# Pre-LN attention block with an fp8 linear layer: first batch's stacks by half heads, the second batch's projections inside the first batch's scores, one load behind the maxima's rows, and one sum of the tail moved from GpSimd to VectorE

## The chip, the cores and the metric

The kernel runs on one core of a Trainium2 chip. The metric is the device time of one execution in microseconds (us), the median of three runs. Engines are named as in the profile: PE is TensorE, PEld its weight loads, DVE is VectorE, ACT is ScalarE, POOL is GpSimd, SP is SyncE, which only issues DMAs here; SPq and ACTq are the issuing queues of SP and ACT.

## The reference

16 sequences of 512 tokens and 256 channels, 16 heads of 16 channels, all float32:

```
x = x + attention(layernorm(x))          # qkv projection, softmax(q k / 4) v, output projection
x = x + linear(fp8(layernorm(x)))        # input clipped to +-448 and rounded to fp8 e4m3, 256 x 256 weight, bias
```

## The kernel before, in words

**Slots and steps.** The work is a pipeline of batches: slot `u` prepares batch `u` (and x of batch `u+1`), runs the scores of batch `u-1`, finishes the exponentials and values of batch `u-2` and the linear layer of batch `u-3`. A slot has 32 steps `s`, written out by hand in each engine's program (PE L671, ACT L893, DVE L1122); tuples at the top of the file say at which step each side job stands (`PROJECT_QK_1`, `VALUES_AND_X`, `LN1_SUM`, `TRANSPOSE_MAX` and so on). Each engine runs its list in order, so a wait holds all that stands behind it.

**One step.** PE makes two score matmuls with queries on the partitions (`scores`, L628, into `ps_s[s % 2]`). DVE takes their maximum along the keys (`maxima`, L1013). After every 8 steps PE transposes these maxima (`transpose_max`, L534), DVE splits them into two rows (L1060, L1062), and SP copies them as two further contraction rows into the q stack (`rows`, L343: four DMAs of 4 KB). Half a slot later PE computes the same scores with keys on the partitions and the maximum already subtracted (`scores_t`, L609, into the two banks of `ps_t`), ACT takes their exponential into `pt` (L797), and PE multiplies with the values (`values`, L649) in every odd step. The scores of step `s` may start once the maxima of step `s-2` are done; `scores_t` of a bank may start once the exponential of the step before has read it.

**Precision by parts.** Projections are three products of high and low parts (6 matmuls for 128 columns). Q and K of a batch lie in `parts[:, n]`, n = 0 to 3: q and k of heads 0 to 7 (n = 0, 1) and of heads 8 to 15 (n = 2, 3). ACT takes n from its bank (L851), POOL splits it into high and low parts (L1330, L1332), and SP copies it into the `qs`/`ks` stacks by six DMAs of 128 KB (`stack`, L334). In the first batch, ACT (L848) and DVE (L1000) split, and n = 0 and 1 are copied by half heads with `copy_first` (L249, 64 KB each): the first four scores pairs need the semaphore `first_stack[0]`, 12 such DMAs. SP issues all of Q's, both halves of it, and K's second half (its `first_slot`); ACT issues K's first half, six DMAs (`stack_k`, L863), ahead of its copies of n = 2 and 3.

**Slot 0 on PE** (L494): transposes of x(0), `project_first` for n = 0 to 3, values of batch 0 (L515), then a wait until DVE has the last low part and ACT the values (`low_ready` 4, `v_ready` 4), 5 unread matmuls that only keep the engine busy (L506), and the 8 transposes of x(1) into `ps_o` and `ps_t` (L450). Then slot 1 begins. In its steps 0 to 15 there are no `scores_t`, only the scores of batch 0; one to three unread matmuls (L709) and one projection matmul of batch 1 (L464, `PROJECT_QK_1`) stand in each. n = 2 and 3 of batch 1 follow in steps 16 to 19 with three matmuls a step, all into the one bank `ps_m`. The values of batch 1 and the transposes of x(2) (`values_and_x`, L515 and L527) stand in steps 20, 22, 24 and 26. `scores_t` of batch 0 starts at step 16 and needs the rows of steps 0 to 7 (`rows_in[0]`).

**Layernorm of x(2)**: DVE takes the sums (L1020) and moments (L1026 to L1030) in slot 0, before the first maxima; POOL takes the power and normalises x(2) (`layernorm_x`, L1287, L1298) early in slot 1, before its splits of batch 1. In all later slots the sums stand at steps 5, 7, 10, 12 and 13.

**SP in slot 1**: the load of x(3) (L314), rows 0, stack n = 0, stack n = 1, rows 1, stacks n = 2 and 3, rows 2. ACT issues the six K DMAs of heads 8 to 15 of batch 0 (L889) at the end of its slot 0.

**The tail** (`finish`): the last batch is rounded to fp8 on DVE in three pieces of 2, 1 and 1 token blocks (`LAST_PIECES`), five DVE operations a piece (L1250 to L1260); each piece is transposed by PE (L770), copied by ACT (L947), multiplied by PE (L780); then DVE scales and adds (L1266) and SP stores. POOL adds the second half of the batch before (L1465, two operands in SBUF, 128x512) once ACT has scaled it (L938).

Of the kernel before, what the change touches and what calls it, by code (L numbers as in the profile page):

```python
# [5 lines left out]
F32 = mybir.dt.float32  # L6
# [48 lines left out]
PROJECT_QK_1 = (range(4, 10), range(10, 16), (16, 17), (18, 19))  # L55
# [9 lines left out]
LN1_END = 13  # L65
LN2_SUM = (31, 31, 1, 2)
# [5 lines left out]
WARM_STEPS = (2, 2, 2, 2, 1, 1, 1, 1, 3, 1, 1, 1, 1, 1, 1, 1)  # L72


def block_kernel(nc, x, qkv_wT, qk_bT, v_bT, proj_wT, proj_b, lin_wT, lin_b, in_scale, w_scale, eye, out):
# [4 lines left out]
    with ExitStack() as ctx:  # L80
# [181 lines left out]

        def sum_bank(half):

            return (ps_o, ps_m)[half][:].rearrange("p (j d) -> p j d", j=2)
# [26 lines left out]
        def _(sp):  # L292
# [58 lines left out]
            def first_slot():  # L351

                load(2, 0)
                sp.wait_ge(ones, 1)
                for par in range(2):
                    for g in range(2):
                        rows = slice(HALF * g + KR, HALF * g + KM)
                        sp.dma_start(ks[par][rows, :, :].bitcast(F32),
                                     nmax[:].rearrange("p t i m -> p (t i m)")).then_inc(ks_ones, 16)
                for half in range(2):  # L360
                    sp.wait_ge(whole_ready, 1)
                    for r in (0, 1):
                        copy_first(sp, qs, 0, Q_PARTS, r, half)
                    sp.wait_ge(low_ready, 1)
                    copy_first(sp, qs, 0, Q_PARTS, 2, half)
                sp.wait_ge(low_ready, 2)
                for r in (0, 2, 1):
                    copy_first(sp, ks, 1, K_PARTS, r, 1)
                stack(0, 0, 2)

            def slot(u, par, present):
                if u == 0:
                    first_slot()
                    return
# [12 lines left out]
                if present(2, B - 1):  # L387
                    reload(u - 2, par)
                if present(3) and u < LAST_SLOT:
                    store(u - 3, 0)  # L390
                if present(1):
                    rows(u - 1, 1 - par, 1)
                if present(3) and u < LAST_SLOT:
                    store(u - 3, 1)
                if present(0):
                    stack(u, par, 2)
                    stack(u, par, 3)
                if present(1):
                    rows(u - 1, 1 - par, 2)
# [17 lines left out]
        def _(pe):  # L417
# [35 lines left out]
            def project_qk(u, n, part, parts):  # L453

                bank = ps_m[:]
                if part == 0:
                    take_bank("project_qk", n, u)
                    if n == 0:
                        pe.wait_ge(xnT_low, 2 * u + 2)
                first = (n % 2) * D + (n // 2) * P  # L460
                products = [(pw, px, c) for pw, px in PAIRS for c in range(NC)]
                for m in range(6 * part // parts, 6 * (part + 1) // parts):
# [27 lines left out]
            def first_slot():  # L490
# [142 lines left out]
            def values(b, par, n, a):  # L633

                t, odd, kp = n // 4, n // 2 % 2, n % 2
                if a == 0:
                    if n == 0:
                        pe.wait_ge(v_ready, NJ * b + NJ)

# [15 lines left out]
            def slot(u, par, present):  # L655
# [3 lines left out]
                for s in range(STEPS):  # L659
# [11 lines left out]
                    if s in TRANSPOSE_MAX[:3] and present(1):  # L671
                        transpose_max(u - 1, TRANSPOSE_MAX.index(s))
                    if u == 1 and s < len(WARM_STEPS):
                        unread(WARM_STEPS[s])
# [10 lines left out]
                    if s in VALUES_AND_X and present(0):  # L685
                        values_and_x(u, VALUES_AND_X.index(s))
# [19 lines left out]
            def unread(count):  # L706

                for i in range(count):
                    nc.tensor.matmul(ps_t[:, 1, :], wqkv_p[:, 0, 0, 0:P], wqkv_p[:, 0, 0, 0:S], start=True, stop=True)  # L709
# [78 lines left out]
        def _(act):  # L788
# [48 lines left out]
            def copy_qk(b, par, n):  # L837

                t, bias = n // 2, bias_column(b, n)
                bank = ps_s[:, n // 2, n % 2, :] if isinstance(b, int) and b == 0 else ps_m[:]  # L840
# [22 lines left out]
            def stack_k(half):  # L863

                act.wait_ge(whole_ready, 2)
                for r in (0, 2):
                    copy_first(act, ks, 1, K_PARTS, r, half)
                act.wait_ge(low_ready, 2)
                copy_first(act, ks, 1, K_PARTS, 1, half)

            def first_slot():
# [6 lines left out]
                stack_k(0)  # L878
# [4 lines left out]
                for c in range(NC):  # L883
                    copy_xnT(1, c)
                act.wait_ge(low_ready, 4)
                for r, part in enumerate(K_PARTS):
                    for g in range(2):
                        rows = slice(HALF * g + HD * r, HALF * g + HD * (r + 1))
                        act.dma_start(ks[0][rows, NS:2 * NS, :].bitcast(F32),  # L889
                                      parts[HALF * g:HALF * (g + 1), 3, part, :]).then_inc(stacked[1][0], 16)  # L890

            def slot(u, par, present):
# [3 lines left out]
                for s in range(STEPS):  # L896
# [14 lines left out]
                    if s in VALUES_AND_X and present(0):  # L911
                        copy_v(u, par, VALUES_AND_X.index(s))
                        if u < B - 1:
                            copy_x_half(u + 1, VALUES_AND_X.index(s))
# [49 lines left out]
        def _(dve):  # L964
# [5 lines left out]
            def prepare():  # L970
# [33 lines left out]
                for j in range(NJ):  # L1004
                    ln1_sum(2, 0, j)
                ln1_finish(2)
# [126 lines left out]
            def slot(u, par, present):  # L1133
                for s in range(STEPS):
# [54 lines left out]
            def finish(b):  # L1189
# [71 lines left out]
                for n, (low, high) in enumerate(LAST_PIECES):  # L1261
# [5 lines left out]
                                             in1=h[:, tok, :], op0=ALU.mult, op1=ALU.add).then_inc(y_ready, 1)  # L1267

# [11 lines left out]
        def _(pool):  # L1280
# [112 lines left out]
            def slot(u, par, present):  # L1393
# [3 lines left out]
                if u == 1:  # L1397
# [3 lines left out]
                    layernorm_x(2, 0)  # L1401
# [16 lines left out]
                if present(-1) and u != 1:  # L1418
# [37 lines left out]
            def finish(b):  # L1456
                for half in range(2):
# [47 lines left out]
```

## Time and profile before

| | |
|---|---|
| median of 3 runs | 931.93 us (931.64 to 932.08) |
| the profiled execution | 932.24 us |
| its span in the trace | 930.4 us |
| PE busy | 912.7 us, 98% of the span |
| DVE, ACT, POOL busy | 836.2, 667.5, 514.4 us (90, 72, 55%) |
| granted TensorE clock | 1.00 of full |
| DMA, mean over the span | 85 GB/s |

The profiled execution is 1.84 us longer than its span (launch and end around it) and 0.31 us above the median. Times in trace rows count from the span's start. "Idle before" names the time that the engine stood still before a row and what released it.

### The profile page before, as it was taken

To read this page: it belongs to the slowest core of one execution; us is meant where nothing else is said; L and a number is where in the kernel's file an instruction comes from. 1 tells how busy PE (TensorE), PEld (TensorE's weight loads), DVE (VectorE), ACT (ScalarE), POOL (GpSimd) and SP (SyncE) were. 2 spreads that over 40 slices of the span, in tenths; PEclk is the share of its full clock that TensorE was granted. 3 is DMA by queue.
4 is the path that set the end of the run, shared out by engine and by line. 5 is a ranking of instruction groups with operands and counts; after the bars stand their busy time and mean duration, and the time that the engine had idled before them with its cause. 6 is when DMAs were issued, how large, how long until landed. Compare 5 with 4: busy or idle time off the path is not lost.

```text
span 930.4 us, 17052 instructions
## 1 busy us (share of the span) xinstructions
PE 912.7 (98%) x5901; PEld 434.3 (47%) x5901; DVE 836.2 (90%) x1264; ACT 667.5 (72%) x1294; POOL 514.4 (55%) x528
## 2 busy tenths in 40 slices
PE   7999999999999999999999999999999999998997
PEld 5444444445444454544445444444544445443336
DVE  6978899898999989899998989999898998899986
ACT  3277767777776777777777777777777677776784
POOL 4533449285573937638294664829556492833433
PEclk9999999999999999999999999999999999999999
DMA  7864607556281644718355380745538064470101
GB/s 199 139 104 85 100 25 132 74 76 111 52 142 38 120 66 79 127 37 144 52 104 81 66 143 24 143 66 91 93 59 142 10 127 59 66 118 3 47 1 47
DMA packets 46206, 78.92 MB, mean 85 GB/s; under 512 B 10088, under 2 KB 13288, under 8 KB 46120
## 3 DMA queue, kind: packets, MB, share of 16 engines
q1 hardware_dynamic: 45352, 76.65, 46.7%
q10 hardware_dynamic: 768, 1.18, 0.8%
q8 instruction: 47, 0.77, 0.4%
q14 instruction: 39, 0.32, 0.1%
HBM read 17.90 MB, written 8.39 MB: 28 GB/s over the span
## 4 chain that ended last, share of the span: by engine, by line
PE 93%; DVE 3%; ACT 2%; DMA 1%; issue 1%; SPq 0%; POOL 0%; ACTq 0%; DVEq 0%; POOLq 0%
PE ps_t L609 28%; PE ps_o L649 27%; PE ps_m L464 10%; PE ps_s L628 8%; PE ps_m L515 6%; PE ps_m L550 5%; PE ps_m L584 3%; ACT pt L797 2%; PE ps_s L534 1%; PE ps_m L527 1%; DVE mx L1013 1%; PE ps_m L567 1%; PE ps_s L486 1%; DMA qs<-nmax 1%; DMA xin<-in_x 0%
## 5 line engine op out<-in xcount | busy, mean ns | idle before, releaser
L797 ACT ACTIVATE pt<-ps_t 128x512 f32<-128x512 f32 x1008 | 548.8, 599 | 187.5 <-PE ps_t L609 183.6
L1013 DVE TENSOR_REDUCE mx<-ps_s 128x2 f32<-128x1024 f32 x512 | 611.5, 1207 | 43.0 <-PE ps_s L628 40.9
L609 PE MATMUL ps_t<-qs,ks 50*128 50x512 f32 x1008 | 375.5, 449 | 7.0 <-ACT pt L797 6.8
L628 PE MATMUL ps_s<-ks,qs 48*128 48x512 f32 x1024 | 375.1, 450 | 0.0
L609 PEld LDWEIGHTS ps_t<-qs,ks 50*128 50x128 f32 x1008 | 159.8, 184 | 286.4 <-ACT pt L797 206.0
L649 PE MATMUL ps_o<-pt,vt 128*32 128x512 f32 x2048 | 272.4, 604 | 0.0
L1341 POOL TENSOR_TENSOR on<-ot,rden 128x256 f32<-128x256 f32 x63 | 39.1, 621 | 225.5 <-DVE rden L1074 225.5
L628 PEld LDWEIGHTS ps_s<-ks,qs 48*128 48x128 f32 x1024 | 158.4, 184 | 6.6 <-DVE mx L1013 4.0
L464 PE MATMUL ps_m<-xnT_p,wqkv_p 128*128 128x512 f32 x360 | 109.1, 420 | 0.1
L1332 POOL TENSOR_TENSOR parts<-parts 128x512 f32<-128x512 f32 x60 | 81.6, 1360 | 4.9
L649 PEld LDWEIGHTS ps_o<-pt,vt 128*32 128x32 f32 x2048 | 40.5, 108 | 88.2 <-issue 81.8
L464 PEld LDWEIGHTS ps_m<-xnT_p,wqkv_p 128*128 128x128 f32 x360 | 60.9, 188 | 33.7 <-issue 25.2
L1316 POOL TENSOR_TENSOR oT_p<-oT,oT_p 128x512 fp32r<-128x512 f32 x31 | 39.7, 1280 | 47.0 <-ACT oT_p L835 47.0
L851 ACT ACTIVATE parts<-ps_m,b_qk 128x512 f32<-128x512 f32 x60 | 41.3, 688 | 30.7 <-PE ps_m L464 30.6
L515 PE MATMUL ps_m<-wqkv_p,xnT_p 128*128 128x256 f32 x360 | 58.1, 296 | 0.1
L550 PE MATMUL ps_m<-wproj_p,oT_p 128*128 128x256 f32 x360 | 54.2, 293 | 0.0
L515 PEld LDWEIGHTS ps_m<-wqkv_p,xnT_p 128*128 128x128 f32 x360 | 46.2, 188 | 14.8 <-issue 14.3
L550 PEld LDWEIGHTS ps_m<-wproj_p,oT_p 128*128 128x128 f32 x360 | 45.5, 189 | 10.1 <-issue 10.1
L1308 POOL CAST xnT_p<-xn 128x512 fp32r<-128x512 f32 x30 | 18.4, 612 | 54.5 <-PE ps_m L515 52.0
L1070 DVE STREAM_TRANSPOSE ot<-ps_o 128x512 f32<-128x512 f32 x63 | 44.2, 702 | 1.4 <-PE ps_o L649 1.4
L1330 POOL CAST parts<-parts 128x512 fp32r<-128x512 f32 x60 | 36.6, 609 | 14.6 <-ACT parts L851 14.6
L1372 POOL TENSOR_TENSOR hn<-hn,xres 128x1024 f32<-128x1024 f32 x14 | 33.3, 2381 | 12.8 <-DVE xres L1102 12.8
(145 smaller groups left out, 836.3 us busy)
## 6 DMA issues: line engine op xcount, KB each, us to landing
qs<-parts SPq DMA_DIRECT2D x186, 128.0 KB, 4.4
ks<-parts SPq DMA_DIRECT2D x180, 128.0 KB, 5.2
xin<-in_x SPq DMA_DIRECT2D x16, 512.0 KB, 3.6
xres<-in_x SPq DMA_DIRECT2D x15, 512.0 KB, 5.7
out<-h SPq DMA_DIRECT2D x29, 256.0 KB, 2.6
qs<-nmax SPq DMA_DIRECT2D x256, 4.0 KB
pt<-in_qkv_wT SPq DMA_DIRECT2D x1, 768.0 KB, 5.2
qs<-parts SPq DMA_DIRECT2D x12, 64.0 KB, 3.4
```

The costliest lines, as they stand in the source:

```text
L464: last = nc.tensor.matmul(bank, wqkv_p[:, pw, c, first:first + P], xnT_p[:, px, c, :], start=m == 0, stop=m == 5)
L515: last = nc.tensor.matmul(bank, xnT_p[:, px, c, tok], wqkv_p[:, pw, c, 2 * D:3 * D], start=(m == 0 and c == 0), stop=(m == 2 and c == NC - 1))
L550: last = nc.tensor.matmul(bank[:, j * D:(j + 1) * D], oT_p[:, px, t, tok], wproj_p[:, pw, t, :], start=(m == 0 and t == 0), stop=(m == 2 a ...
L609: nc.tensor.matmul(t_bank(b, s, g), ks[par][rows, slot, keys], qs[par][rows, slot, :], start=True, stop=True).then_inc(st_done, 1)
L628: done = nc.tensor.matmul(ps_s[:, s % 2, g, :], qs[par][rows, slot, queries], ks[par][rows, slot, :], start=True, stop=True)
L649: last = nc.tensor.matmul(ps_o[32 * i:32 * i + VW, :], vt[par][:, 2 * kp + a, head, :], pt[n % 2][:, i, a, :], start=(kp == 0 and a == 0), ...
L797: nc.scalar.activation(pt[n % 2][:, w % 2 + 2 * a, w // 2, :], t_bank(b, s, a), ACT.Exp, scale=SCALE).then_inc(exp_done, 1)
L851: nc.scalar.activation(parts[:, n, 1, :], bank, ACT.Identity, bias=bias).then_inc(whole_ready, 1)
L1013: dve.tensor_reduce(mx[:, r, :, s % QUARTER], ps_s[:, s % 2, :, :], AX_X, ALU.max).then_inc(max_done, 1)
L1070: dve.transpose(ot[:].rearrange("p a c -> p (a c)"), ps_o[:]).then_inc(ot_ready, 1)
L1316: pool.tensor_tensor(oT_p[:, 1, t, :], oT[:], oT_p[:, 0, t, :].bitcast(F32), ALU.subtract).then_inc(oT_low, 1)
L1332: pool.tensor_tensor(parts[:, n, 1, :], parts[:, n, 1, :], parts[:, n, 0, :], ALU.subtract).then_inc(low_ready, 1)
```

## The change

Steps and banks of slot 1: batch 1's projections get three steps of two matmuls each in steps 5 to 16, by turns into `ps_m` and `ps_o`, with the products ordered by the half of x that they need; the transposes of x(1) move from the end of slot 0 into steps 1 and 2; `values_and_x` moves to 22, 24, 26, 28; unread matmuls in slot 1 fall from 22 to 11. The 5 unread matmuls of slot 0 write `ps_o` and no longer wait. ACT's first-half K copy shrinks from six DMAs to two, and SP issues the other four, after Q's first half and ahead of Q's second; ACT's K copies of the second heads follow its copy of the transposed x(1). The sums for x(2) move on DVE from slot 0 to steps 15 to 19 of slot 1, and POOL's normalising of it behind its four splits. SP takes rows 0 ahead of the load of x(3). In the tail DVE makes the sum of L1465 after its first piece. Only slots 0 and 1 and the tail are touched.

```diff
-PROJECT_QK_1 = (range(4, 10), range(10, 16), (16, 17), (18, 19))
+PROJECT_QK_1 = ((5, 6, 7), (8, 9, 10), (11, 12, 13), (14, 15, 16))
+TRANSPOSE_X_1 = (1, 2)
+VALUES_AND_X_1 = (22, 24, 26, 28)
+LN1_SUM_1 = (15, 16, 17, 18)
+LN1_END_1 = 19
-WARM_STEPS = (2, 2, 2, 2, 1, 1, 1, 1, 3, 1, 1, 1, 1, 1, 1, 1)
+WARM_STEPS = (2, 0, 0, 2, 2, 0, 0, 0, 1, 0, 0, 0, 0, 0, 0, 4)
...
+        def qk_bank(b, n):
+
+            if b == 0:
+                return ps_s[:, n // 2, n % 2, :]
+            return ps_o[:] if b == 1 and n % 2 else ps_m[:]
...
-                for half in range(2):
-                    sp.wait_ge(whole_ready, 1)
-                    for r in (0, 1):
-                        copy_first(sp, qs, 0, Q_PARTS, r, half)
-                    sp.wait_ge(low_ready, 1)
-                    copy_first(sp, qs, 0, Q_PARTS, 2, half)
+                sp.wait_ge(whole_ready, 1)
+                for r in (0, 1):
+                    copy_first(sp, qs, 0, Q_PARTS, r, 0)
+                sp.wait_ge(low_ready, 1)
+                copy_first(sp, qs, 0, Q_PARTS, 2, 0)
                 sp.wait_ge(low_ready, 2)
+                copy_first(sp, ks, 1, K_PARTS, 1, 0)
+                copy_first(sp, ks, 1, K_PARTS, 2, 0)
+                for r in (0, 1, 2):
+                    copy_first(sp, qs, 0, Q_PARTS, r, 1)
                 for r in (0, 2, 1):
                     copy_first(sp, ks, 1, K_PARTS, r, 1)
                 stack(0, 0, 2)
...
+                if u == 1:
+                    rows(0, 0, 0)
                 if present(-2):
                     load(u + 2, par)
-                if u == 1:
-                    rows(0, 0, 0)
...
-                bank = ps_m[:]
+                bank = qk_bank(u, n)
                 if part == 0:
-                    take_bank("project_qk", n, u)
-                    if n == 0:
+                    if u > 1 or n % 2 == 0:
+                        take_bank("project_qk", n, u)
+                    if u > 1 and n == 0:
                         pe.wait_ge(xnT_low, 2 * u + 2)
+                    if u == 1 and n == 1:
+                        pe.wait_ge(xnT_ready, 6)
+                    if u == 1 and n == 3:
+                        pe.wait_ge(whole_ready, 4 + 2)
...
+                    if u == 1 and n == 0 and m % 3 == 0:
+                        pe.wait_ge(xnT_low, 2 + c + 1)
...
-                pe.wait_ge(low_ready, 4)
-                pe.wait_ge(v_ready, 4)
                 for i in range(WARM_SCORES):
-                    nc.tensor.matmul(ps_s[:, 1, 1, :], wqkv_p[:, 0, 0, 0:P], wqkv_p[:, 0, 0, 0:S], start=True, stop=True)
-                for c in range(NC):
-                    transpose_x(1, c)
+                    nc.tensor.matmul(ps_o[:], wqkv_p[:, 0, 0, 0:P], wqkv_p[:, 0, 0, 0:S], start=True, stop=True)
...
+                    if u == 1 and s == TRANSPOSE_X_1[1]:
+                        pe.wait_ge(v_ready, 4)
+                    if u == 1 and s in TRANSPOSE_X_1:
+                        transpose_x(1, TRANSPOSE_X_1.index(s))
...
-            def stack_k(half):
+            def stack_k():
 
                 act.wait_ge(whole_ready, 2)
-                for r in (0, 2):
-                    copy_first(act, ks, 1, K_PARTS, r, half)
-                act.wait_ge(low_ready, 2)
-                copy_first(act, ks, 1, K_PARTS, 1, half)
+                copy_first(act, ks, 1, K_PARTS, 0, 0)
...
+                    if u == 1 and s in TRANSPOSE_X_1:
+                        copy_xnT(1, TRANSPOSE_X_1.index(s))
+                    if u == 1 and s == TRANSPOSE_X_1[1]:
+                        stack_second_k()
...
                 finish_bias()
-                for j in range(NJ):
-                    ln1_sum(2, 0, j)
-                ln1_finish(2)
...
-                    if present(-1) and u > 1:
-                        if s in LN1_SUM:
-                            ln1_sum(u + 1, 1 - par, LN1_SUM.index(s))
-                        if s == LN1_END:
+                    if present(-1) and u > 0:
+                        steps_sum, step_end = (LN1_SUM_1, LN1_END_1) if u == 1 else (LN1_SUM, LN1_END)
+                        if s in steps_sum:
+                            ln1_sum(u + 1, 1 - par, steps_sum.index(s))
+                        if s == step_end:
                             ln1_finish(u + 1)
...
+                    if n == 0:
+                        dve.wait_ge(lin_scaled, 1)
+                        dve.tensor_tensor(y_before[:, 2:4, :], y_before[:, 2:4, :], xin[0][:, 2:4, :],
+                                          ALU.add).then_inc(y_before_ready, 1)
...
                     split_lin()
-                    layernorm_x(2, 0)
...
-                if present(-1) and u != 1:
+                if present(-1):
                     layernorm_x(u + 1, 1 - par)
...
-                pool.wait_ge(lin_scaled, 1)
-                pool.tensor_tensor(y_before[:, 2:4, :], y_before[:, 2:4, :], xin[0][:, 2:4, :],
-                                   ALU.add).then_inc(y_before_ready, 1)
```

## Rows read from the trace of the kernel before

**Rows 1.** The page's chain that ended last, share by engine

```profile
PE 93%; DVE 3%; ACT 2%; DMA 1%; issue 1%; SPq 0%; POOL 0%; ACTq 0%; DVEq 0%; POOLq 0%
```

**Rows 2.** Timeline of PE, end of slot 0: start us, us, instruction, idle before

```profile
17.39 3.15 PE L515 MATMUL ps_t<-wqkv_p,xnT_p 128*128 128x256 f32 x24
21.36 1.39 PE L506 MATMUL ps_s<-wqkv_p 128*128 128x512 f32 x5 [0.81 <-ACT vt L811]
...
23.55 0.50 PE L628 MATMUL ps_s<-ks,qs 48*128 48x512 f32 x2
```

**Rows 3.** Timeline of SP: DMA issues in slots 0 and 1

```profile
13.50 7.60 SPq L249 DMA_DIRECT2D qs<-parts  x12
...
25.10 5.59 SPq L334 DMA_DIRECT2D qs<-parts  x6
```

**Rows 4.** Tile ks: ACT's last two issues of K's first half, at 17.6 and 18.3

```profile
DMA to landing us min/median/max: 4.2/4.7/5.2
```

**Rows 5.** Tile ks, 21.0 to 22.5 us: three issues of SP, ACT issuing none

```profile
DMA to landing us min/median/max: 2.7/2.8/3.0
```

**Rows 6.** Tile qs: SP's last issue of the second heads' Q, at 29.8

```profile
DMA to landing us min/median/max: 9.5/9.5/9.5
```

**Rows 7.** Chain in order of time: the wait for the rows of steps 0 to 7

```profile
36.47 6.04 DMA qs<-nmax
```

**Rows 8.** Timeline of DVE, slots 0 and 1

```profile
21.66 1.41 DVE L1020 BATCH_NORM_STATS2 st<-xin 128x6 f32<-128x256 f32 x4 [0.26 <-POOL xn L1298]
...
23.70 0.15 DVE L1030 TENSOR_REDUCE ve<-mv 128x4 f32<-128x8 f32 x1
24.10 9.14 DVE L1013 TENSOR_REDUCE mx<-ps_s 128x2 f32<-128x1024 f32 x8 [0.25 <-PE ps_s L628]
...
43.62 0.28 DVE L1060 TENSOR_SCALAR nmax<-ps_s 16x128 fp32r<-16x128 f32 x1 [0.37 <-PE ps_s L534]
...
44.15 2.33 DVE L1013 TENSOR_REDUCE mx<-ps_s 128x2 f32<-128x1024 f32 x2
```

**Rows 9.** Timeline of POOL, slot 1: normalising x(2)

```profile
30.80 1.02 POOL L1287 TENSOR_TENSOR rs<-ve,half_neg 128x4 f32<-128x4 f32 x1
32.15 2.16 POOL L1298 TENSOR_SCALAR xn<-xin,nm,rs 128x256 f32<-128x256 f32 x4 [0.33 <-POOL rs L1287]
```

**Rows 10.** Timeline of PE: first scores_t of steps 23, 26, 28 and 30 of slot 1

```profile
54.62 0.50 PE L609 MATMUL ps_t<-qs,ks 50*128 50x512 f32 x1
...
59.75 0.50 PE L609 MATMUL ps_t<-qs,ks 50*128 50x512 f32 x1
...
63.19 0.50 PE L609 MATMUL ps_t<-qs,ks 50*128 50x512 f32 x1
...
66.36 0.50 PE L609 MATMUL ps_t<-qs,ks 50*128 50x512 f32 x1
```

**Rows 11.** Timeline of the tail: DVE, POOL and PE around the second and third pieces

```profile
919.63 0.69 DVE L1258 TENSOR_TENSOR hn<-hn,parts 128x512 f32<-128x512 f32 x1
...
921.36 1.36 POOL L1465 TENSOR_TENSOR parts<-parts,xin 128x512 f32<-128x512 f32 x1 [2.09 <-ACT parts L938]
...
921.62 1.26 DVE L1255 TENSOR_SCALAR parts<-parts 128x256 f32<-128x256 f32 x1
...
924.36 0.29 DVE L1255 TENSOR_SCALAR parts<-parts 128x256 f32<-128x256 f32 x1
...
923.88 0.29 PE L770 MATMUL ps_t<-ident_b,hq 128*128 128x128 bf16 x2
924.63 0.74 PE L780 MATMUL ps_s<-wlin_p,hqT 128*128 128x256 f32 x4 [0.46 <-ACT hqT L947]
925.63 0.28 PE L770 MATMUL ps_t<-ident_b,hq 128*128 128x128 bf16 x2 [0.27 <-DVE hq L1260]
...
927.15 0.48 DVE L1266 SCALAR_TENSOR_TENSOR h<-ps_s,s_in,h 128x256 f32<-128x256 f32 x1 [0.53 <-PE ps_s L780]
```

**Rows 12.** Windows: us, busy (x) of PE, PEld, DVE, ACT, POOL, clock, DMA

```profile
66.00:69.00 3.00, 2.56 (x20) 0.83 (x16) 2.34 (x3) 2.06 (x5) 0.00 (x0) 1.00 0.00 0
```

More of the change, by code:

```diff
@@ L638, in values @@
                         pe.wait_ge(v_ready, NJ * b + NJ)
+                    if n == 0 and b == 0:
+                        pe.wait_ge(whole_ready, 4 + 4)
                     early = 2 if b == B - 1 and n == UNITS - 1 else 0
@@ L672, in slot @@
                         transpose_max(u - 1, TRANSPOSE_MAX.index(s))
+                    if u == 1 and s == TRANSPOSE_X_1[1]:
+                        pe.wait_ge(v_ready, 4)
+                    if u == 1 and s in TRANSPOSE_X_1:
+                        transpose_x(1, TRANSPOSE_X_1.index(s))
                     if u == 1 and s < len(WARM_STEPS):
-                        unread(WARM_STEPS[s])
+                        unread(WARM_STEPS[s], ps_o[:] if s == 0 else ps_t[:, 1, :])
                     for j in range(2):
@@ L684, in slot @@
                         linear(u - 3, LINEAR.index(s))
-                    if s in VALUES_AND_X and present(0):
-                        values_and_x(u, VALUES_AND_X.index(s))
+                    steps_vx = VALUES_AND_X_1 if u == 1 else VALUES_AND_X
+                    if s in steps_vx and present(0):
+                        values_and_x(u, steps_vx.index(s))
                     if s in PROJECT_OUT[0] and present(2, B - 1):
@@ L704, in bias, with unread @@
                 last.then_inc(bias_done, 1)
-            def unread(count):
+            def unread(count, bank=ps_t[:, 1, :]):
                 for i in range(count):
-                    nc.tensor.matmul(ps_t[:, 1, :], wqkv_p[:, 0, 0, 0:P], wqkv_p[:, 0, 0, 0:S], start=True, stop=True)
+                    nc.tensor.matmul(bank, wqkv_p[:, 0, 0, 0:P], wqkv_p[:, 0, 0, 0:S], start=True, stop=True)
             def project_last(bank, t, half, picks):
@@ L839, in copy_qk @@
                 t, bias = n // 2, bias_column(b, n)
-                bank = ps_s[:, n // 2, n % 2, :] if isinstance(b, int) and b == 0 else ps_m[:]
+                bank = qk_bank(b, n)
                 act.wait_ge(qk_done, 4 * b + n + 1)
@@ L861, in copy_hqT, with stack_second_k @@
                                bank.bitcast(BF16).rearrange("p (c n) -> p c n", c=NC)[:, :, tok]).then_inc(hqT_ready, 1)
-            def stack_k(half):
+            def stack_k():
                 act.wait_ge(whole_ready, 2)
-                for r in (0, 2):
-                    copy_first(act, ks, 1, K_PARTS, r, half)
-                act.wait_ge(low_ready, 2)
-                copy_first(act, ks, 1, K_PARTS, 1, half)
+                copy_first(act, ks, 1, K_PARTS, 0, 0)
+            def stack_second_k():
+                act.wait_ge(low_ready, 4)
+                for r, part in enumerate(K_PARTS):
+                    for g in range(2):
+                        rows = slice(HALF * g + HD * r, HALF * g + HD * (r + 1))
+                        act.dma_start(ks[0][rows, NS:2 * NS, :].bitcast(F32),
+                                      parts[HALF * g:HALF * (g + 1), 3, part, :]).then_inc(stacked[1][0], 16)
             def first_slot():
@@ L877, in first_slot @@
                 copy_qk(0, 0, 1)
-                stack_k(0)
+                stack_k()
                 copy_qk(0, 0, 2)
@@ L882, in first_slot @@
                 copy_first_v(1)
[L883 to L890, printed above, removed]
             def slot(u, par, present):
@@ L910, in slot @@
                             copy_hqT(u - 3, half)
-                    if s in VALUES_AND_X and present(0):
-                        copy_v(u, par, VALUES_AND_X.index(s))
+                    if u == 1 and s in TRANSPOSE_X_1:
+                        copy_xnT(1, TRANSPOSE_X_1.index(s))
+                    if u == 1 and s == TRANSPOSE_X_1[1]:
+                        stack_second_k()
+                    steps_vx = VALUES_AND_X_1 if u == 1 else VALUES_AND_X
+                    if s in steps_vx and present(0):
+                        copy_v(u, par, steps_vx.index(s))
                         if u < B - 1:
-                            copy_x_half(u + 1, VALUES_AND_X.index(s))
+                            copy_x_half(u + 1, steps_vx.index(s))
             def copy_sum(b, half):
```

2 lines of the change are left out of this document (added).

## The prediction

> **What bounds the kernel now.** I read the page first: the chain that ended last is 93% PE [rows 1], so what the opening gives is kept to the end if slot 2 begins earlier, and what the tail gives comes on top. Then the timelines of PE, DVE and SP in the first 70 us, because the change touches only slots 0 and 1 and the tail. The reader is to see three stretches with different limits. From 20.54 (17.39 + 3.15) to 23.55 us PE has little to do but wait, pad and transpose [rows 2]. In steps 0 to 15 DVE sets the pace: eight maxima take 9.14 us, 1.14 each, back to back [rows 8]. From step 20 on PE does, with pairs of steps of 3.44 us where `values_and_x` stands in one (59.75 to 63.19) and 3.17 us where it doesn't (63.19 to 66.36) [rows 10].
>
> **The opening.** Before, the first scores start at 23.55 [rows 2]. Two things end just then: PE's transposes of x(1), and the last DMA of K's first half, issued by ACT at 18.3 and landed up to 5.2 us later, at 23.5 [rows 4]. So taking PE's wait and the transposes away would alone bring nothing; the DMAs must land earlier too. After, PE runs its 5 unread matmuls right behind 20.54: 1.39 us, free at about 21.85. SP begins at 13.50 and needs 7.60 / 12 = 0.633 us an issue [rows 3]. Of its first ten DMAs (six of Q, four of K) the last starts at 13.50 + 9 x 0.633 = 19.2. ACT's two are the first of its former six, whose last stood at 17.6 and 18.3 [rows 4]: they land long before. What that tenth DMA takes to land is unknown: 2.7 to 3.0 us where SP issues alone [rows 5], 4.2 to 5.2 where two queues fill the DMA engines [rows 4]. After the change SP is alone from 16 us on, so I take 2.8: landing at 22.05, first scores at 22.1, 1.45 us earlier. The bounds are 21.85 (PE's padding ends it, 1.7 us) and 19.2 + 4.2 = 23.4 (0.15 us).
>
> The Trainium skill (DMA: Bandwidth & Descriptors, "Anatomy of one DMA") puts the fixed part of a DMA at about 2.0 us, measured for GpSimd's path. By it, as an estimate, the tenth would land near 21.4 and the padding would decide; the trace's shortest here is 2.7.
>
> **Steps 0 to 15.** Every step still has about four matmuls' time on PE or less, so DVE's pace stays: from 24.10 to the end of the sixteenth maxima at 43.25 (43.62 less 0.37 idle) are 19.15 us [rows 8]. After: 22.65 to 41.8. The two transposes of x(1) in steps 1 and 2 are covered by DVE; the split x(1) is then ready just before steps 5 and 6 want its two halves, by my estimate with under 1 us to spare, and if that goes, PE's lead of two steps over DVE pays it first. 11 unread matmuls fewer save nothing, since PE waited for DVE there anyway. The four projections land in `ps_m` and `ps_o` by turns; a copy on ACT fits into the three steps, 3.4 us, between them.
>
> **Step 16.** Before, scores_t waits for the rows of steps 0 to 7: issued by 36.47, landed 6.04 us later [rows 7], behind the load of x(3). It costs nothing beyond 0.2 us, since the transpose of the maxima behind it waits for maxima 15 anyway. After, PE wants these rows and the second heads' stacks at about 40.8, free until 41.05. SP begins the second heads' Q at 19.8 + 12 x 0.633 = 27.4 instead of 25.10, issues for 3.8 to 5.6 us [rows 3] and before needed 9.5 us to land [rows 6], with the load of x(3) behind it and ACT's six beside it. That gives 39.5 to 41.7, centre 40.5; the rows follow within some tenths. I take nothing, and keep 0.7 us for the range. The load of x(3), then K and Q of batch 1 wait on SP behind the rows until about 35.6; all are wanted in slot 2, which begins after 66.36 [rows 10]: covered by 25 us and more.
>
> The Trainium skill (DMA: Bandwidth & Descriptors, "Queues, rings and completion order") says that a DMA's semaphore is written only after all earlier writes of that DMA engine, of any queue. By it the 4 KB rows cannot overtake the stacks, so the reorder would be worth only the load's part; the 6.04 us of rows 7 agree with that.
>
> **Steps 16 to 22.** Here the change puts work on DVE: four sums of 1.41 / 4 = 0.35 us, and moments of 0.8 us (23.07 to 23.85) [rows 8]; the sums stood in idle time before. The first sum hides in the 0.37 us before the split. From the end of maxima 15 at 41.8: split and restart 0.9 (43.25 to 44.15), four maxima 4 x 1.16 = 4.65, three sums 1.05, moments 0.8 = 49.2. PE has only four matmuls in steps 17 to 20, so DVE is the bound. Then POOL's power, gap and normalising, 3.5 us (30.80 to 34.31) [rows 9]: x(2) is ready at 52.85. PE reaches the transposes of x(2) in step 22 at about 52.0 (maxima 20 end at 50.35, scores and projections 1.6), so a **new wait of about 0.85 us** stands there, of PE on POOL. With the 0.2 us of transposes step 23 begins at 53.1 instead of 54.62 [rows 10]: **1.5 us earlier**. Without the wait it would be 2.3.
>
> **Steps 23 to 31.** The fourth `values_and_x` now stands in step 28, so that pair takes 3.44 instead of 3.17 us [rows 10]: 0.27 us lost. Slot 2 begins **1.2 us earlier**. POOL's split of x(2) starts behind step 28 instead of 26; PE wants it four steps (over 6 us) behind step 30: hidden. Slots 2 to 17 are unchanged and PE-bound.
>
> **The tail.** DVE's L1255 takes 1.26 us at 921.62 while POOL's sum runs from 921.36 to 922.72, and 0.29 at 924.36 [rows 11]: DVE was held for 0.97 us. With the sum gone from POOL, the second piece is rounded 0.97 us earlier. But PE comes to it at 923.88 with no wait, straight from its own matmuls [rows 11], so that piece doesn't move. The third piece's transposes start at 925.63, after an idle 0.27 (weight loads 0.47); after, they follow the matmuls of 924.63 + 0.74 directly, at about 925.2. So **0.4 us** come through, with 0.27 and 0.97 as ends. The sum on DVE costs 0.69 (the 128x512 sum at 919.63) and lies between the first and the second piece's last operation, from about 925.3 to 926.0; the second then ends at 926.45 and the third isn't wanted before 926.8: hidden by 0.35 us.
>
> **The sum**: 1.5 - 0.27 + 0.4 = 1.6 us. The profiled execution of 932.24 becomes 930.6; the median is 0.31 below it, so **930.3 us**, 0.17% less. About 0.2% (1.86 us) is what a measurement of this kernel can tell from no change.
>
> **Rivals.** *Late stacks.* The tenth DMA lands as those that shared the engines did, in 4.2 us [rows 4]: the opening gives 0.15 instead of 1.45, and the time is 931.6. Or the second heads' stacks land at 41.7: step 16 waits 0.65 beyond what is free, 931.0. The two don't add, since a late opening moves step 16 back too. For it: ACT's and SP's issues of the second heads still run together. Against: ACT's queue is empty when the tenth goes out.
> *More comes through.* The padding ends the opening (0.25 more), PE's matmuls in the tail move up and the whole 0.97 comes (0.57 more), or DVE's sums fit beside the scores (up to 0.8 more): 929.4 with two of them. For it: the first DMAs with SP alone landed in 2.7 [rows 5]. Against: PE comes to 923.88 with no idle time before it [rows 11].
> *The clock falls* (slower). Steps 17 to 20 leave PE busy 1.0 us in 1.5, and then comes the wait of step 22. If the granted clock goes to 1.2 GHz, one PE-bound pair of steps at that level costs 3.44 us more: 933.7. It decides from the point where the granted clock in 43 to 53 us falls under 1.00 for more than about 1.6 us of matmuls. Against: it is 1.00 at 66 to 69 us, with 2.56 of 3 us busy [rows 12], and nothing in the opening drops it. The Trainium skill (TensorE: Matmul & The Clock Gate, "A second HAM failure mode: psum-queue depth-cycling") says that frequent small idles between groups of matmuls can make the clock oscillate; this trace shows no such case.
> *It doesn't do what it says*: the first scores start where they did since transposes and DMAs only swap the last place; then 931.6, the far end of the first rival and counted with it.
>
> **How the numbers follow.** Forecast as worked out 0.56; late stacks 0.22, at 931.0 to 931.6; more comes through 0.16, around 929.4; clock or another loss of that kind 0.06, 933.7. The range from 929.3 to 931.9 takes in the first three with the spread of the runs shown (0.3 below and above at most), and leaves out the last. Faster by over 0.2% needs 930.07: the third case and a fifth of the first, 0.27. Slower by over 0.2% needs 933.8, about what the last gives: 0.07 with a hundredth for other losses. The rest, 0.66.
>
> **What would show it.** First scores at 22.1; maxima 15 end at 41.8; a wait of PE on POOL's L1298 of 0.5 to 1 us at step 22; step 23 at 53.1; step 30 at 65.2 instead of 66.36; no POOL in the tail and L1255 at 0.3 three times; the last PE transposes directly behind matmuls. Wrong if step 16 waits on a DMA past 41.1, if the first scores stand after 23, or if any window of slot 1 shows a clock under 1.00.

## The result, and the profile after

| | before | changed |
|---|---|---|
| median of 6 runs | 931.96 us (931.48 to 939.57) | 942.44 us (935.63 to 944.47) |
| ratio to before | | 1.0083, 95% interval 1.0046 to 1.0119 |
| profiled execution, its span | 932.24, 930.4 us | 942.83, 941.0 us |
| granted clock, mean over the span | 1.00 | 0.983 |

The change makes the kernel slower by 0.8%, where 0.17% faster was forecast. The changed kernel's six took 935.63 to 944.47 us, the two shortest (935.63 and 937.08) at a mean clock of 0.992 and 0.990, the other four at 0.982 to 0.985; only the profiled one of 942.83 has a trace. Single executions scatter, of the kernel before too (27 of its 123 in all took 937 to 950 us, at a mean clock of 0.977 to 0.994), and since the ratios are averages, which such executions raise, they can lie below 1 where median and lowest both lie above (e2, e5): so below the lowest time stands beside each median.

The page of the changed kernel, part 2: the line of PE's busy share and of the clock, 23.5 us a digit.

```profile
PE   7899999999999999999999999999999999999998
...
PEclk9669999999999999999999999999999999999999
```

The clock is low in the second and third slice alone, so I read slot 1 by windows (columns as in [rows 12], behind the clock the DMA share and GB/s):

```profile
20.00:30.00 10.00, 10.00 (x47) 5.32 (x45) 7.77 (x7) 1.76 (x3) 6.73 (x11) 1.00 0.66 121
31.50:51.50 20.00, 17.03 (x38) 7.95 (x38) 10.61 (x11) 2.06 (x3) 5.67 (x7) 0.50 1.04 150
53.00:58.00 5.00, 4.21 (x17) 1.88 (x16) 4.98 (x8) 4.70 (x9) 1.89 (x2) 1.00 0.05 8
59.00:68.00 9.00, 9.00 (x35) 3.43 (x35) 5.03 (x8) 3.66 (x8) 3.19 (x5) 0.50 1.06 133
69.50:80.00 10.50, 10.05 (x74) 5.03 (x72) 8.77 (x11) 8.60 (x20) 2.69 (x4) 1.00 0.02 4
```

The granted clock is 0.50, that is 1.2 GHz, for 20 us and, behind steps 17 to 20 (PE busy 4.21 of 5 us from 53 to 58), once more for about 10. PE's timeline over the places that answer to [rows 2] and [rows 10] shows what stood ahead of the first fall:

```profile
20.45 1.30 PE L526 MATMUL ps_o<-wqkv_p 128*128 128x512 f32 x5
21.68 0.50 PE L646 MATMUL ps_s<-ks,qs 48*128 48x512 f32 x2
...
29.62 0.74 PE L486 MATMUL ps_m<-xnT_p,wqkv_p 128*128 128x512 f32 x2
34.47 0.80 PE L646 MATMUL ps_s<-ks,qs 48*128 48x512 f32 x2 [4.12 <-DMA ks<-parts]
...
36.80 0.79 PE L646 MATMUL ps_s<-ks,qs 48*128 48x512 f32 x2
...
38.67 0.79 PE L646 MATMUL ps_s<-ks,qs 48*128 48x512 f32 x2
...
51.62 0.61 PE L627 MATMUL ps_t<-qs,ks 50*128 50x512 f32 x1
...
65.02 0.79 PE L627 MATMUL ps_t<-qs,ks 50*128 50x512 f32 x1
```

The first scores do come early, at 21.68. But at step 8 PE stands still for 4.12 us, until 34.47, for **K's second half of the first heads** (`first_stack[1]`). The scores wait in step `s` for `first_stack[s // 8]`: not the first four pairs but steps 0 to 7 need the first half, and step 8 is the first to need the second. The clock drops during that wait, 1.1 us after PE ran dry, and the steps behind it take 1.87 us (36.80 to 38.67) instead of 1.14. SP's timeline answers to [rows 3]:

```profile
13.56 3.79 SPq L253 DMA_DIRECT2D qs<-parts  x6
17.40 2.49 SPq L253 DMA_DIRECT2D ks<-parts  x4
19.93 3.76 SPq L253 DMA_DIRECT2D qs<-parts  x6
23.74 4.23 SPq L253 DMA_DIRECT2D ks<-parts  x6
28.17 3.80 SPq L344 DMA_DIRECT2D qs<-parts  x6
36.30 3.14 SPq L353 DMA_DIRECT2D qs<-nmax  x4
```

Tile ks, SP's last two issues of that half, and how long they took to land:

```profile
L253 SPq DMA_DIRECT2D ks<-parts x2: 594/594/595, 26.7 to 27.4; - x2
...
DMA to landing us min/median/max: 6.1/6.6/7.1
```

ACT's queue at that time, from its timeline:

```profile
25.00 3.94 ACTq L899 DMA_DIRECT2D ks<-parts  x6
```

The last two of that half in the kernel before:

```profile
L249 SPq DMA_DIRECT2D ks<-parts x2: 592/593/594, 23.7 to 24.3; - x2
...
DMA to landing us min/median/max: 3.1/3.6/4.0
```

So K's second half, four issues later on SP than before, now runs beside ACT's six DMAs of 128 KB each, and its last lands 7.1 us behind its issue instead of 4.0. The account against the kernel before, by PE's starts: first scores 1.9 us ahead (21.68 against 23.55), step 8 2.2 behind (34.47 against 32.29), step 16 9.1 behind (51.62 against 42.55), step 23 10.4 behind (65.02 against 54.62), step 30 12.4 behind (78.81 against 66.36). Of these 12.4 about 1 comes back in the slots behind, most of which take 55.00 us instead of 55.06 (from a row of PE to the same row a slot later), and 0.8 in the tail: 10.6 in the span.

### The profile page after: what moved, and what is told of

It reads as the page before. It is cut to its first block, busy times and chain, and to the rows that moved or that the text cites. A ratio compares the mean times of both kernels' runs of the same rounds, so it can differ in the third digit from the quotient of the medians.

```text
span 941.0 us, 17029 instructions
## 1 busy us (share of the span) xinstructions
PE 920.7 (98%) x5890; PEld 438.1 (47%) x5890; DVE 836.1 (89%) x1265; ACT 668.2 (71%) x1294; POOL 513.8 (55%) x527
## 4 chain that ended last, share of the span: by engine, by line
PE 94%; ACT 2%; SPq 1%; DVE 1%; DMA 1%; issue 1%; POOL 0%; ACTq 0%; DVEq 0%; POOLq 0%
PE ps_t L627 28%; PE ps_o L669 27%; PE ps_m L486 10%; PE ps_s L646 9%; PE ps_m L533 6%; PE ps_m L568 5%; PE ps_m L602 3%; SPq L253 1%; PE ps_s L552 1%; PE ps_m L545 1%; ACT pt L822 1%; PE ps_m L585 1%; DMA ks<-parts 1%; DVE mx L1038 1%; PE ps_o L486 1%
## 5 line engine op out<-in xcount | busy, mean ns | idle before, releaser
L1038 DVE TENSOR_REDUCE mx<-ps_s 128x2 f32<-128x1024 f32 x512 | 612.3, 1207 | 49.9 <-PE ps_s L646 48.1
L486 PE MATMUL ps_m<-xnT_p,wqkv_p 128*128 128x512 f32 x348 | 106.4, 427 | 0.0
L1085 DVE TENSOR_SCALAR nmax<-ps_s 16x128 fp32r<-16x128 f32 x64 | 17.6, 275 | 30.9 <-PE ps_s L552 30.9
```

The source lines that it names most:

```text
L1038: dve.tensor_reduce(mx[:, r, :, s % QUARTER], ps_s[:, s % 2, :, :], AX_X, ALU.max).then_inc(max_done, 1)
```

## The experiments

All runs start from the changed kernel unless said otherwise; "before" is the kernel before, measured beside the run on the same chip. Times in us: median, lowest.

| run | median | lowest | before: median, lowest | ratio (interval) |
|---|---|---|---|---|
| e1_old_split | 936.12 | 931.41 | 932.84, 931.84 | 1.0025 (0.9987 to 1.0064) |
| e2_late_second_k | 934.20 | 934.09 | 932.84, 931.84 | 0.9990 (0.9957 to 1.0023) |
| e3_bridge | 935.49 | 934.83 | 932.84, 931.84 | 1.0015 (0.9987 to 1.0044) |
| e4_tail_alone | 932.34 | 931.26 | 932.84, 931.84 | 0.9989 (0.9960 to 1.0017) |
| e5_bridge_pad | 934.05 | 933.64 | 933.13, 932.11 | 0.9990 (0.9963 to 1.0017) |
| e9_slot1_alone | 934.95 | 932.83 | 933.13, 932.11 | 1.0006 (0.9974 to 1.0039) |
| e10_slot1_pad | 933.07 | 931.81 | 933.13, 932.11 | 1.0004 (0.9966 to 1.0042) |
| e8_tail_rows | 932.50 | 931.33 | 933.13, 932.11 | 0.9977 (0.9950 to 1.0005) |
| e6_late_pad | 935.54 | 934.43 | 932.75, 931.61 | 1.0020 (1.0003 to 1.0038) |
| e11_act_half2_pad | 930.33 | 929.37 | 932.75, 931.61 | 0.9981 (0.9955 to 1.0007) |
| e12_act_half2 | 932.78 | 930.47 | 933.31, 932.13 | 0.9989 (0.9973 to 1.0005) |
| e13_again | 930.46 | 929.84 | 933.31, 932.13 | 0.9960 (0.9941 to 0.9979) |

**The late half, and who makes it late.** Run e2: ACT waits with its six.

```diff
-                    if u == 1 and s == TRANSPOSE_X_1[1]:
-                        stack_second_k()
+                    if u == 1 and s == 3:
+                        act.wait_ge(first_stack[1], 192)
+                        stack_second_k()
```

> The change, but ACT issues its six K DMAs of the second heads only when K's second half of the first heads has landed. Theory L: these six took the DMA engines from K's second half; without them it lands by 31 (issued to 27.5, about 3 us), step 8 waits under 1 us, and the clock stays at 1.00 through step 8. The second heads' stacks then land later, near 41, so step 16 may wait up to 2 us. 929.5 to 933. Rival (the half is late because SP issues it last, whoever shares the engines): it lands past 33 and step 8 waits 2 us or more. Rival S: a fall of the clock in steps 17 to 20 whatever step 8 does, 934 or more.

Tile ks of this run, SP's last two issues of K's second half:

```profile
L253 SPq DMA_DIRECT2D ks<-parts x2: 592/592/592, 27.9 to 28.5; - x2
...
DMA to landing us min/median/max: 2.3/2.3/2.3
```

They land in 2.3 us instead of up to 7.1, and step 8 has no wait. (All of this trace stands 1.0 to 1.5 us later, PE and SP alike, because its clock was low for a time already in slot 0; see the last section.) So ACT's six held the half up, not its place in SP's queue by itself. But the six now start at 30.8, and the wait moves on to step 16. PE's timeline:

```profile
44.46 0.49 PE L627 MATMUL ps_t<-qs,ks 50*128 50x512 f32 x1 [1.66 <-DMA qs<-nmax]
```

The rows of the maxima, 4 KB each, issued by 36.9, land at 44.4, behind the stacks issued before them. That the stacks hold them up is argued from this order; e11 below, which issues the same stacks earlier, has no such wait. Then the clock falls at 45.6, to 55.8, that is 1.1 us after this wait of 1.66 us and before the sparse steps 17 to 20. All ten executions lie between 934.1 and 935.7.

**The wait and the clock apart.** Run e3: PE bridges the wait with unread matmuls.

```diff
-WARM_STEPS = (2, 0, 0, 2, 2, 0, 0, 0, 1, 0, 0, 0, 0, 0, 0, 4)
+WARM_STEPS = (2, 0, 0, 2, 2, 0, 0, 20, 1, 0, 0, 0, 0, 0, 0, 4)
```

> The change with 20 unread matmuls (some 4.3 us) behind step 7, which fill PE's wait for K's second half. What L and the clock cost apart: the wait stays (scores of step 8 at about 34.5), but the clock should stay at 1.00 there. If the fall at 31 us is the larger part of the loss, steps 8 to 15 take 1.15 us each instead of 1.87 and the time falls by 6 us, to some 935 to 937 with a second fall in steps 17 to 20 (S), or to 932.5 to 934 without one (L alone). If the time stays at 942, the clock does not go by PE's idle stretch.

K's half is no earlier (step 8 at 35.06, the 20 matmuls taking about as long as the wait did), yet 7 of the 10.5 us are gone. Windows of this run:

```profile
36.00:40.00 4.00, 3.92 (x17) 1.66 (x15) 3.96 (x6) 0.69 (x1) 2.18 (x3) 1.00 1.08 131
40.00:44.00 4.00, 4.00 (x15) 1.79 (x16) 4.00 (x4) 0.69 (x1) 2.46 (x4) 1.00 0.98 219
...
48.00:52.00 4.00, 3.50 (x13) 1.69 (x13) 4.00 (x6) 3.58 (x8) 1.50 (x2) 0.96 1.06 155
52.00:56.00 4.00, 4.00 (x14) 1.20 (x15) 3.13 (x9) 1.51 (x3) 2.69 (x5) 0.50 0.89 166
```

The clock stays at 1.00 over step 8 and falls behind steps 17 to 20, where PE has four matmuls a step. Run e5 fills those steps too:

```diff
+                    if u == 1 and s in (18, 19, 20):
+                        if s == 18:
+                            pe.wait_ge(whole_ready, 8)
+                        unread(2, ps_o[:])
```

> The run with 20 unread matmuls behind step 7, plus two unread matmuls in each of steps 18, 19 and 20. With the bridge alone the clock stayed at 1.00 to 51.5 us and then fell, after steps 17 to 20 with four matmuls each. Theory S2: those sparse steps are what drops the clock the second time. Then here it is 1.00 through slot 1, and the time is 1.5 to 3 us under the bridge's 935.5: 932.5 to 934, the wait at step 8 being all that is left. Rival: it falls there whatever PE does (a late effect of the wait): again near 51, 935 to 936.

1.00 from 20 to 80 us, mean clock 0.996 to 1.000 in all ten executions (e3: 0.992 to 0.996), 1.4 us less than e3 (1.2 by the lowest). The sparse steps are the second cause. What is left is the late half without the clock: 0.9 us (median) to 1.5 us (lowest) above the kernel before, what the rest of the change gains already taken off.

**The opening undone.** Run e1 puts the stack DMAs of the first batch back and keeps PE's early unread matmuls:

```diff
-                copy_first(act, ks, 1, K_PARTS, 0, 0)
+                for r in (0, 2):
+                    copy_first(act, ks, 1, K_PARTS, r, 0)
+                act.wait_ge(low_ready, 2)
+                copy_first(act, ks, 1, K_PARTS, 1, 0)
```

(and SP's loop over both halves as before)

> The change with the first batch's stack DMAs put back: ACT issues K's first half (six DMAs), SP both halves of Q, then K's second half. Theory L (late half): the changed kernel loses by K's second half alone, which lands at 34.4 us, so step 8 waits 4.1 us and the clock falls behind it. Then here the first scores stand at 23.6, step 8 has no wait on a DMA, the clock is 1.00 to 52 us at least, and the time is 930 to 932. Rival S (sparse steps): the clock falls because PE's work was thinned (11 unread matmuls fewer, four matmuls a step in steps 17 to 20). Then it falls here too, in steps 17 to 20 at 55 us or so, and the time is 935 or more. Both may hold: no wait at step 8 and yet a fall later.

A miss, and a telling one. PE's timeline, in the profiled execution of 948.03 us:

```profile
20.51 1.30 PE L523 MATMUL ps_o<-wqkv_p 128*128 128x512 f32 x5
24.57 0.79 PE L643 MATMUL ps_s<-ks,qs 48*128 48x512 f32 x2 [2.75 <-DMA ks<-parts]
25.30 1.22 PE L731 MATMUL ps_o<-wqkv_p 128*128 128x512 f32 x2
```

PE is done early and then idles 2.75 us, and the clock is gone from the first scores on (0.50 from 24.2 to 58.3 us). 4 of the 12 executions took 931.4 to 932.3, 8 took 935.1 to 948.0. In the kernel before, the wait that the change removed from slot 0 (`low_ready`, `v_ready`, 0.81 us) and the transposes of x(1) behind the padding (0.96 us) keep PE busy until 23.55, close to where the DMAs land; here both are gone from that place, and the DMAs landed about 1 us later besides. Which of the three weighs most was not taken apart. Run e9 restores all of slot 0 and its DMAs (with two unread matmuls in each of steps 0 to 4), and keeps the later steps of slot 1; e10 adds the padding of e5 to it.

> The change without anything in the opening: stack DMAs, the wait, the padding and the transposes of x(1) as in the kernel before; the steps of slot 1 (projections by twos in 5 to 16, sums in 15 to 19, values at 22 to 28, rows ahead of the load) and the tail as changed. Theory: the opening holds the large loss, so no wait at step 8 and first scores at 23.6 or a little later; S2 says that the clock falls once, near 49 us, behind steps 17 to 20: 932.5 to 935. If S2 is wrong: 930.5 to 931.5.

> The same with two unread matmuls in each of steps 18 to 20. S2: no fall, and the moved projections, the moved sums and the tail show what they are worth by themselves: 930.5 to 931.5, the wait of PE for the normalised x(2) at step 22 included. Rival: 932 or more, if the padding or that wait takes all back.

e9: one fall of the clock in slot 1, in steps 17 to 20 as expected (clock 0.80 in 48 to 52 us, 0.50 to 56), 934.95. e10: 933.07 and 931.81 at the lowest, against 933.13 and 932.11: better than e9 by 1.0 to 1.9 us, but not clearly better than before. Steps of slot 1 and tail together are worth 0.1 to 0.3 us when the clock is held, no more than the tail gives alone in e4: no gain of the moved steps by themselves is shown. Three executions of e10 took 940.1 to 945.6 all the same; the profiled one, of 945.62, waited 1.66 us for the first stack, and its clock was at 0.50 from 26.0 to 56.8 us.

**The tail and the rows.** e4 has only DVE's sum of the tail; e8 has it and SP's rows ahead of the load; both start from the kernel before.

> The kernel before with the tail's part alone: the sum on VectorE behind its first piece. My sum: 0.4 us, 931.5; the last PE transposes start directly behind the matmuls before. The rival of the whole 0.97 us: 931.0. Nothing else moves.

> The kernel before with two parts of the change: the tail's sum on VectorE, and SP's rows ahead of the load of x(3). In the kernel before the rows landed at 42.51, just when step 16 wanted them. Theory D (DMA volume): they land behind what was issued before them, so without the load ahead they land 1 to 3 us earlier and step 16 has no wait: 0 to 0.3 us, with the tail's 0.4: 931.2 to 931.6. Rival: nothing from the rows, 931.6.

Timeline of PE in e4, its tail, to compare with [rows 11]:

```profile
924.47 0.29 PE L770 MATMUL ps_t<-ident_b,hq 128*128 128x128 bf16 x2
925.21 0.74 PE L780 MATMUL ps_s<-wlin_p,hqT 128*128 128x256 f32 x4 [0.46 <-ACT hqT L947]
925.79 0.28 PE L770 MATMUL ps_t<-ident_b,hq 128*128 128x128 bf16 x2
```

From the second piece's transposes to the third's are 1.32 us instead of 1.75 (923.88 to 925.63): the 0.4 us. From DVE's last operation to the end of the span are 2.4 us instead of 2.8, which I had not counted (every trace with DVE's sum has it, 2.4 us), so the trace shows 0.8. In the times it is 0.5 to 0.6 (median and lowest), inside the scatter. e8's lowest lies 0.8 under before, no more than e4's can be told from it: what the rows bring by themselves stays open.

**A version that beats both.** SP alone leaves the DMA engines half idle (share 0.46 in 20 to 24 us in the changed kernel). So ACT issues K's second half there, and SP comes to the second heads 3.8 us sooner.

```diff
                 copy_first_v(0)
+                act.wait_ge(low_ready, 2)
+                copy_first(act, ks, 1, K_PARTS, 0, 1)
                 copy_first_v(1)
+                copy_first(act, ks, 1, K_PARTS, 2, 1)
+                copy_first(act, ks, 1, K_PARTS, 1, 1)
...
-                for r in (0, 2, 1):
-                    copy_first(sp, ks, 1, K_PARTS, r, 1)
```

e6, the other repair, is e2 with the padding; e12 is e11 without the padding; e13 is e11 again.

> The run in which ACT issues the second heads' K only after K's second half has landed, plus two unread matmuls in each of steps 18 to 20. That run had no wait at step 8, one of 1.7 us at step 16, and a clock at 1.2 GHz from 46 to 55 us: 934.2. If the sparse steps drop the clock (S2), it is 1.00 throughout here and 1.5 to 2.5 us come back: 931.7 to 932.7. If the wait at step 16 drops it, the clock falls again at 46 us and the time stays near 934. And since first scores here wait for no DMA, no execution should lie near 940.

> The changed kernel, but ACT issues K's second half of the first heads (six DMAs, between and behind its copies of the values, from 19.9 us), so that SP comes to the second heads' Q 3.8 us earlier; with two unread matmuls in each of steps 18 to 20. If the DMA engines' idle half between 20 and 28 us is what the changed kernel wastes, K's second half lands by 29, step 8 has no wait, the second heads' stacks land by 40 and step 16 has next to none: 930.0 to 931.3, and no execution near 940, the first version that beats both. Rival: the volume of the stacks sets step 16 whoever issues them: rows land at 42 or later and the time is 931.5 to 932.5.

> The changed kernel with the one repair alone: ACT issues K's second half, no extra unread matmuls in steps 18 to 20. The theory has two causes: the late half (repaired here) and the sparse steps. So no wait over 1 us at step 8, the clock at 1.00 to 47 us, then one fall behind steps 17 to 20: 931.5 to 933.5, mean clock 0.994 to 0.996 in nearly every execution. If the late half were the only cause, 930.3 as with the padding.

> The version with ACT issuing K's second half and two unread matmuls in steps 18 to 20, a second time, for its interval: it gave 930.33 us against 932.75. Again 929.3 to 931.9 with at most one or two executions near 940, 0.2 to 0.3% under the kernel before; if it was chance, within 0.1%.

e6 missed: 935.54, 1.3 us more than e2, its twin without the padding (chips differ). It waits 2.29 us at step 16, the clock falls 2.7 us after that wait, and then the padding costs time:

```profile
48.00:52.00 4.00, 4.00 (x12) 1.78 (x10) 3.54 (x5) 2.20 (x5) 1.08 (x1) 0.50 1.09 130
```

PE is busy throughout at half clock, and the scores of steps 18 to 21 start 2.3 us apart (47.60, 49.96, 52.26, 54.56); in e2, at half clock too, they start 1.5 apart (47.55, 49.02, 50.50, 51.98). The fall is not all of it: two executions of e6 had a mean clock of 0.998 and took 935.39 and 936.22.

e11 and e13 hit: 930.33 and 930.46, 2.4 and 2.9 us under the kernel before by the median and 2.2 and 2.3 by the lowest. The interval of e13 lies wholly below 1 (0.9941 to 0.9979), that of e11 reaches 1.0007; 1 of their 24 executions took over 937. PE's timeline of e11:

```profile
22.10 0.50 PE L644 MATMUL ps_s<-ks,qs 48*128 48x512 f32 x2 [0.39 <-DMA ks<-parts]
...
30.80 0.50 PE L644 MATMUL ps_s<-ks,qs 48*128 48x512 f32 x2
...
41.61 0.50 PE L625 MATMUL ps_t<-qs,ks 50*128 50x512 f32 x1
...
52.88 0.44 PE L543 MATMUL ps_m<-ident,xn 128*128 128x128 f32 x2 [0.80 <-POOL xn L1334]
53.25 0.49 PE L625 MATMUL ps_t<-qs,ks 50*128 50x512 f32 x1
```

First scores at 22.10, step 8 at 30.80 behind at most 0.4 us of waiting, step 16 at 41.61, PE's wait for the normalised x(2) of 0.80 us. e12: 932.78, mean clock 0.992 to 0.996 in all twelve, against 0.995 to 1.000 in e13, measured beside it: the padding of steps 18 to 20 is worth 2.3 us by the median (0.6 by the lowest), and the late half is not the only cause.

## Why the prediction was wrong

- **The step that failed** is "Steps 0 to 15: DVE's pace stays". I followed SP's queue to its tenth DMA and then to the second heads. I counted the twelve issues between, but did not ask when the last six of them, K's second half, land, for which step 8 waits. They start at 23.74 instead of 21.14 and collide with ACT's six; PE stood still for 4.12 us there. The numbers were at hand: 19.8 + 6 x 0.633 = 23.6 for the first, 26.8 for the last, and the slow landings of two queues together, 4.2 to 9.5 us [rows 4, 6]: an arrival between 31.0 and 36.3, against a want at 30.3. The last took 7.1.
- **The clock** stood among the rivals with 0.06 and one pair of steps, 3.44 us. It was the larger part: of the 10.5 us, e3 gives 7 back without making the DMA earlier. "Nothing in the opening drops it" fell with the step above: the wait at step 8 did. My evidence against it [rows 12] had PE busy 2.56 of 3 us; steps 17 to 20 of e12 have 3.42 of 4, no less, and it fell all the same. A busy share of one window is not the measure. The removal of 11 unread matmuls I costed at nothing, which holds for PE's time and not for what it kept up. The Trainium skill (TensorE: Matmul & The Clock Gate, "A second HAM failure mode: psum-queue depth-cycling"), which I set beside this rival, says that small idles between groups of matmuls can make the clock oscillate. The traces agree as far as one fall goes: with idles of 0.19 to 0.39 us from 44.2 to 46.6 the clock of e12 fell at 48.1, and in e11 and e13, where unread matmuls stand in those steps, it stayed at 1.00.
- **The opening** was right: forecast 22.1, measured 21.68 (PE's padding, my other bound, 21.85) and in e11 22.10. In the changed kernel the tenth DMA lands in 2.2 us, where I took 2.8.
- **Step 16** was mis-sized: I took nothing, with the second heads' Q landing at 39.5 to 41.7. In the changed kernel it landed at about 42.0:

```profile
L344 SPq DMA_DIRECT2D qs<-parts x2: 595/601/607, 30.7 to 31.4; - x2
...
DMA to landing us min/median/max: 10.6/10.6/10.7
```

  That would have cost about 1 us (free until 41.05) had step 8 been on time, an estimate, since PE came to step 16 only at 51.62. In e2 and e6, where ACT's six start later, it waits 1.7 and 2.3 us for the rows, which land behind the stacks; in e11 there is no wait. The waits agree with what the Trainium skill (DMA: Bandwidth & Descriptors, "Queues, rings and completion order") says: a DMA's semaphore is written only after all earlier writes of that DMA engine. Step 24, which needs the rows of steps 8 to 15, waits 1.25 us in e2 and 0.82 in e13; the prediction does not look at it.
- **Steps 16 to 23** were right where the clock holds: a wait of 0.80 us on POOL's L1334 in e11 (forecast 0.85, though 49.2 + 3.5 is 52.7 and not 52.85, which makes it 0.7), step 23 at 53.25 (forecast 53.1).
- **The tail**: 0.4 us as worked out, on PE's chain; the end behind DVE's last operation gave as much again.
- The sum, 930.3, is what e11 measures, 930.33 and 930.46. That is largely luck: e11 has extra padding and DMAs in another order, the kernel before stood at 932.75 and 933.31 beside e11 and e13, so that the gain was 2.2 to 2.9 us and not 1.6, and step 30 came 1.1 us earlier in e11's trace but 0.3 in e13's (forecast 1.2).

## What to carry to other kernels

When DMAs are put ahead of others in a queue, write down every transfer behind them with the step that wants it, up to the last, and look which other queue runs in that window. Unread matmuls cost nothing here while the clock is full and another engine sets the pace (steps 18 to 21 start about 1.45 us apart with them in e11 and without them in e12); at half clock they set the pace themselves (e6). Before any are removed, ask which waits they bridge, and when PE is made free earlier, look whether its padding still ends at the wait (e1). Filling a queue's idle time from a second queue paid where the first left the DMA engines idle (share 0.46 in the changed kernel from 20 to 24 us; e11), and two queues with stacks at once cost time where the engines were full (0.98 from 25 to 34 us in the changed kernel).

## What had not been expected of the hardware

- The clock fell during waits of 4.1 us (changed kernel) and 2.75 us (e1), 1.1 us behind one of 1.66 (e2) and 2.7 us behind one of 2.29 (e6), and without any such wait in or behind steps 17 to 20, with PE busy 3.4 of 4 us (e12, 44 to 48 us; e9, 46 to 50). Once down it stayed for 20 us in steps in which PE was busy all the time by the trace, with four matmuls in 1.87 us, and rose at 51.9, in the changed kernel, behind four unread matmuls and two projections back to back in step 15.
- The kernel before has such a case itself. In one execution of e8, whose slot 0 is that of the kernel before, PE's timeline shows the wait for the first stack:

```profile
25.15 0.49 PE L628 MATMUL ps_s<-ks,qs 48*128 48x512 f32 x2 [1.58 <-DMA ks<-parts]
```

  and the clock is at 0.50 from 28 to 40 us. The wait for the same DMAs was 0.2 us in the profiled execution of before and 0.75 in e4, and there the clock stayed at 1.00. This fits the 27 of 123 long executions; it was seen in that one profile and in e10's, so for the rest it is inferred. It would also give the new opening a worth that the forecast leaves out: with slot 0 as in the kernel before (before, e4, e8, e9, e10) 36 of 171 executions took over 937 us, with the changed opening and the late half bridged or repaired (e2, e3, e5, e6, e11, e12, e13) 4 of 78.
- There is a third place where the clock falls, which no part of the change touches. In the profiled executions of e2, e5, e6 and e9 it was at 0.50 for a time between 9.3 and 16.2 us, and the first scores came 1.2 to 2.8 us later than in a trace without it. Window 10 to 14 us of e5, then of before:

```profile
10.00:14.00 4.00, 3.92 (x12) 2.80 (x11) 2.70 (x4) 1.17 (x2) 0.00 (x0) 0.50 0.66 187
10.00:14.00 4.00, 3.59 (x17) 2.61 (x16) 3.32 (x4) 1.76 (x3) 0.00 (x0) 1.00 0.64 204
```

  PE's wait for the normalised x(0) just before was 1.95 to 2.21 us in e5, e6 and e9 and 1.07 in e2; in the ten other profiles it was 0.86 to 1.87. So an absolute time in one of these four traces cannot be set beside one in another trace, only distances can, and part of the scatter has nothing to do with the change.
- A 4 KB DMA issued by 36.0 us in e6 landed 8.7 us later, behind stacks of 128 KB each.
- The slots behind slot 1 take 0.06 us less each in the changed kernel's trace. It is not the change: with the same code there, e3, e12 and e13 take 55.03 to 55.06 again.
